# Distance products in two row groups of 32 rows instead of one product over 128 rows, with the factors copied to both groups by ScalarE

## The chip, the cores and the metric

The kernel runs on one core of one Trainium2 chip (trn2). The metric is the device time of one execution in microseconds (us). Three runs of the kernel before took 588.64, 587.37 and 587.83 us; their median is 587.83 us.

## The reference

Sixteen graphs of 512 nodes with 128 features go through four graph layers, each followed by a residual sum and a layer norm, `x = layernorm(x + layer(x))`. The layer that matters here is the last one, a gated unit with a neighbourhood built from distances:

```python
s = x @ w_se.T + b_se                                     # 512 x 3 per graph
sq = jnp.sum(s * s, axis=-1)
dist = sq[:, :, None] + sq[:, None, :] - 2.0 * jnp.einsum('bnd,bmd->bnm', s, s)
A = jnp.exp(-dist) * mask                                 # mask is the adjacency
msg = jax.nn.relu(x @ w_msg.T + b_msg)
x_nmp = jnp.einsum('bnm,bmd->bnd', A, msg)
```

Beside it the same layer has a convolution over 17 neighbouring nodes and a gate with three sigmoid and tanh parts. The first layer multiplies by the adjacency (512 x 512), the third by an attention weighted with it.

## The kernel before, in words

A first part works out the second layer for the first 25 nodes of all graphs, and prepares weights. The main part, `turn`, then runs once for each step of a software pipeline: graph g is in its last layer (`cur`), while graph g+1 is in its first and third layer (`nxt`), graph g+2 is loaded and transposed (`new`), and graph g-1 is finished (`prev`). `over_graphs` writes out the first turn and the last ones and makes a hardware loop of two turns a pass of the others. Sixteen turns have `cur`; one more only finishes the last graph. Each engine has its own instruction list, in the order in which it is written, and semaphores tie the lists together (`wait(engine, semaphore, value)`).

Products of full precision are made of three products of float32r operands (`three`, L255 to L259): high times high, high times low and low times high. So most of TensorE's instructions carry the lines L257, L258 and L259.

The distance matrix of a graph, 512 x 512, is four products, one for each chunk `mc` of 128 rows. For these VectorE writes `G` (L1465 to L1477): for each node 13 numbers for the left factor and 13 for the right one, made of the high and the low parts of `s` and of its half squared length, so that the product of the two is minus half the distance. Left and right numbers lie 32 columns apart (`KD` = 13 numbers, `GR` = 32). Four transposing products (L1711) turn `G` into `SQ_BANK`, left factors in partitions 0 to 12 and right factors in partitions 32 to 44. ScalarE copies both to `LR`, to partitions 0 to 12, as left half `LR[:, 0, :]` and right half `LR[:, 1, :]` (L1234, L1235). All other partitions of `LR` were set to zero once, at the start (L1129), and `distances(mc)` (L1604 to L1606) multiplies over all 128 partitions, into `AT_BANK[0]` for even chunks and `AT_BANK[1]` for odd ones.

TensorE's order in one turn around the change is: transposes of `x3`, first aggregation over the adjacency (twelve products of 512 columns), `CONV1`, `hn`, L1684, L1696, L1702, the nine even taps of the convolution (27 products of 256 columns), L1711, nine more taps (27 products), **distances(0) and distances(1)**, six of the eight odd taps (18 products), the second aggregation (twelve products of 512 columns, L1735 to L1740), **distances(2) and distances(3)**, the last two odd taps (6 products), L1752, L1760, transposes of the adjacency, and the gates. In front of the second aggregation TensorE waits for the weighted features of the graph in its third layer: their high part `x_hi` comes from ScalarE (L1243), their low part `x_lo` from VectorE (L1521, L1524), which in its turn needs the chain that begins behind L1684.

ScalarE's order there is: L1228, L1229 (messages), wait for L1711, L1234, L1235, then a wait for VectorE's `ef` and the exponential L1239, four scalings L1243, L1248, and the exponentials of the first two distance products (L1182). VectorE multiplies each exponential by the transposed adjacency (L1354), and TensorE multiplies that by the messages (L1760).

Of the kernel before, what the change touches and what calls it, by code (L numbers as in the profile page):

```python
# [32 lines left out]
KD = 13  # L33
GR = 32
# [4 lines left out]
def network_kernel(nc, a, out):  # L39
# [3 lines left out]
    ACT = mybir.ActivationFunctionType  # L43
# [3 lines left out]
    with ctx:  # L47
        def sb(name, shape, dt=f32):
            return ctx.enter_context(nc.sbuf_tensor(name, shape, dt))

        def sem(name):
            return ctx.enter_context(nc.semaphore(name))
# [14 lines left out]
        AT_BANK = [bank[0], bank[1]]  # L67
# [4 lines left out]
        SQ_BANK = bank[6]  # L72
# [123 lines left out]
        LR = sb("LR", [128, 2, N], f32r)  # L196
# [17 lines left out]
        def ms_banks(nxt):  # L214
            return (MS_BANK if nxt else AG_BANK, AT_BANK[0])

        def ms_half(o):
            return o[:, 0:2 * DM].rearrange("p (c d) -> p c d", c=2)[:, :, 0:D]
# [4 lines left out]
        def wait(eng, s, count):  # L223

            if not (isinstance(count, int) and count <= 0):
                eng.wait_ge(s, count)
# [28 lines left out]
        def three(pe, o, lh, ll, rh, rl, start, stop):  # L255

            nc.tensor.matmul(o, lh, rh, start=start, stop=False)  # L257
            nc.tensor.matmul(o, lh, rl, start=False, stop=False)  # L258
            return nc.tensor.matmul(o, ll, rh, start=False, stop=stop)  # L259

        def ch(c):
            return slice(c * 128, (c + 1) * 128)
# [69 lines left out]
        with nc.Block() as block:  # L332
# [742 lines left out]
        dv_s, dv_ssq, dv_q, dv_shi, dv_qh, dv_G, pe_LR, ac_LR = [sem(n) for n in (  # L1075
            "dv_s", "dv_ssq", "dv_q", "dv_shi", "dv_qh", "dv_G", "pe_LR", "ac_LR")]
# [91 lines left out]
        def _(act):  # L1168
            s = nc.scalar
            def turn(V, dma, par, graph, has, outs):  # L1170
# [48 lines left out]
                if cur:  # L1219
                    wait(act, pe_hn, V(1))  # L1220
                    wait(act, ac_nn, V(0))
                    s.activation(gh, HN_BANK[:, :], ACT.Identity, bias=gate_bias[:, 2:3], scale=0.5).then_inc(ac_gh, 1)
                    wait(act, po_cd, V(1))
                    wait(act, pe_P1, V(0))
                    s.activation(cd_hi[:, :, :], cd[:, :, :], ACT.Identity).then_inc(ac_cdh, 1)
                    wait(act, dv_s, V(1))
                    wait(act, pe_N, V(0))
                    s.activation(msg_v[1], ms_half(ms_banks(nxt)[1]), ACT.Relu).then_inc(ac_msx, 1)  # L1228
                    s.activation(msg_v[0], ms_half(ms_banks(nxt)[0]), ACT.Relu).then_inc(ac_msg, 1)  # L1229
                    wait(act, pe_LR, V(1))  # L1230
                    if not prev:
                        act.wait_ge(po_LR0, 1)
                    wait(act, pe_D[NC - 1], V(0))
                    s.activation(LR[0:KD, 0, :], SQ_BANK[0:KD, :], ACT.Identity)  # L1234
                    s.activation(LR[0:KD, 1, :], SQ_BANK[GR:GR + KD, :], ACT.Identity).then_inc(ac_LR, 1)  # L1235
                if nxt:
                    wait(act, dv_f, V(2))
                    wait(act, dv_pf, V(1))
# [12 lines left out]
                if prev and cur:  # L1251
# [3 lines left out]
                    for c in range(NC):  # L1255
                        last = s.activation(y_out[:, c, :], X_BANK[:, ch(c)], ACT.Identity, bias=shift[:, c:c + 1],
                                            scale=rs[3][:, c:c + 1])
# [31 lines left out]
                if new:  # L1289
                    split_adjacency(3)  # L1290

            over_graphs(act, turn)

        @block.vector
# [292 lines left out]
        def _(pe):  # L1587
            t_ = nc.tensor
            def turn(V, dma, par, graph, has, outs):
# [12 lines left out]
                    return last  # L1602

                def distances(mc):  # L1604
                    t_.matmul(AT_BANK[mc % 2][:, :], LR[:, 0, ch(mc)], LR[:, 1, :], start=True, stop=True  # L1605
                              ).then_inc(pe_D[mc], 1)  # L1606

                def some_taps(o, first, count, hi, lo, ks):
# [24 lines left out]
                if prev and not cur:  # L1633
# [15 lines left out]
                    for h in range(2):  # L1649
                        pe.wait_ge(dv_gy, V(0) + h)  # L1650
                        for c in range(2):
                            last = t_.transpose(Y_HALF[h][:, ch(c)], gy[:, ch(2 * h + c)], ident[:, :])
                        last.then_inc(pe_yT, 1)
                    return
                if cur:
                    wait(pe, dv_x3, V(1))
                    wait(pe, dv_nmplo, V(0))
                    for c in range(NC):
                        last = t_.transpose(X_BANK[:, ch(c)], x3[:, c, :], ident[:, :])  # L1659
# [21 lines left out]
                if nxt:  # L1681
                    wait(pe, ac_agg1, V(2))
                    for c in range(NC):
                        last = t_.matmul(AG_BANK[:, ch(c)], agg_sb[:, ch(c)], w0[:, :], start=True, stop=True)  # L1684
                    last.then_inc(pe_out0, 1)
                if cur:
# [7 lines left out]
                    for c in range(NC):  # L1694
                        o = ms_banks(nxt)[c // 2]
                        last = t_.matmul(o[:, DM * (c % 2):DM * (c % 2) + D + 3], x3M[:, ch(c)], wmsT,  # L1696
                                         start=True, stop=True)
                    last.then_inc(pe_ms, 1)
                if prev and nxt:
                    wait(pe, dv_gy, V(0))  # L1700
                    for c in range(NC):
                        last = t_.transpose(X_BANK[:, ch(c)], gy[:, ch(c)], ident[:, :])  # L1702
                    last.then_inc(pe_yT, 1)
                if cur:
# [5 lines left out]
                    for c in range(NC):  # L1710
                        last = t_.matmul(SQ_BANK[0:2 * GR, ch(c)], G[:, c, :, :].rearrange("p k g -> p (k g)"), ident_r[:, :],  # L1711
                                         start=True, stop=True)
                    last.then_inc(pe_LR, 1)
                if prev and not nxt:
                    wait(pe, dv_gy, V(0))
                    for c in range(NC):
                        last = t_.transpose(X_BANK[:, ch(c)], gy[:, ch(c)], ident[:, :])
# [5 lines left out]
                if cur:  # L1723
                    wait(pe, ac_LR, V(1))
                    wait(pe, ac_msx, V(1))
                    for mc in range(2):
                        if nxt:
                            wait(pe, dv_aTlo[3 - 2 * mc], V(2))
                        wait(pe, dv_P[mc + 2], V(0))
                        distances(mc)  # L1730
                    wait(pe, ac_gh, V(1))
                    some_taps(HN_BANK[:, 0:HALF], EVEN, ODD, cd_hi[:, 1, :], cd_lo[:, 1, :], range(ODD - 2))
                if nxt:
                    wait(pe, dv_pf, V(2))
                    for mc in range(NC):  # L1735
                        wait(pe, ac_xs[mc], V(2))
                        wait(pe, dv_xs[mc], V(2))
                        last = three(pe, AG_BANK[:, :], x_hi[:, mc, :], x_lo[:, mc, :], aT_hi[:, mc, :],
                                     aT_lo[:, mc, :], mc == 0, mc == NC - 1)
                    last.then_inc(pe_agg2, 1)  # L1740
                if cur:
                    for mc in range(2, NC):
                        wait(pe, dv_P[mc - 2], V(1))
                        distances(mc)
                    some_taps(HN_BANK[:, 0:HALF], EVEN, ODD, cd_hi[:, 1, :], cd_lo[:, 1, :], range(ODD - 2, ODD)
                              ).then_inc(pe_P1, 1)
                if nxt:
# [3 lines left out]
                    for c in range(NC):  # L1751
                        last = t_.matmul(OUT2[:, c // 2, c % 2, :], agg_sb[:, ch(c)], wwT, start=True, stop=True)  # L1752
                    last.then_inc(pe_out2, 1)
                if cur:
# [3 lines left out]
                    for mc in range(NC):  # L1758
                        wait(pe, dv_P[mc], V(1))
                        last = t_.matmul(X_BANK[:, :], msg[:, ch(mc)], P[:, mc, :], start=(mc == 0), stop=(mc == NC - 1))  # L1760
# [40 lines left out]
```

## Time and profile before

| | |
|---|---|
| median of three runs | 587.83 us (587.37 to 588.64) |
| the profiled execution | 587.87 us, of which the trace spans 586.1 us |
| TensorE (PE) | 568.1 us busy, 97% of the span |
| weight loads of TensorE (PEld) | 488.0 us |
| VectorE (DVE) | 476.6 us, 81% |
| ScalarE (ACT) | 341.3 us, 58% |
| GpSimd (POOL) | 120.7 us, 21% |

PE rows are products, PEld rows the loads of their stationary operand, which lie beside the product before. A row of the timeline gives a start, the time from the start of its first instruction to the end of its last, engine, line, operation, output <- inputs, rows * columns of the array that are active, the shape and how many instructions were merged into the row (x5). The ends of products are modelled and consecutive products overlap in the record, so what a product costs is read from the distance between starts. For a merged row of n equal products that distance is (length of the row - length of one) / (n - 1).

### The profile page before, as it was taken

Reading aid. Unit: us, or ns where it says so; the run is one execution under the profiler, and the core shown is the slowest. Engines: PE = TensorE matmul, PEld = TensorE weight load, DVE = VectorE, ACT = ScalarE, POOL = GpSimd, SP = SyncE. Lnnn points to the kernel's source line nnn. Section 1 sums busy time; section 2 is a strip of 40 time slices with the busy share of each in tenths; the row PEclk is TensorE's granted clock in tenths of the full one; section 3 lists DMA queues with packets and bytes.
Section 4 is the critical chain, followed back from the end, with each engine's and each line's share of the span. In section 5 each row is a group of like instructions: output and inputs, shape, how many; then the busy total and the mean of one; then the engine's idle time right before and its main releaser. Section 6 shows DMA issues by size and latency. Waiting matters only on the chain.

```text
span 586.1 us, 11733 instructions
## 1 busy us (share of the span) xinstructions
PE 568.1 (97%) x3579; PEld 488.0 (83%) x3579; DVE 476.6 (81%) x1798; ACT 341.3 (58%) x716; POOL 120.7 (21%) x140
## 2 busy tenths in 40 slices
PE   7998999999999999999999999999999999999894
PEld 6896987878979797979888897979797988889684
DVE  4778868888888888888888888888888888888665
ACT  2306646557575656675665757566657566575442
POOL 3310130312213030212131221303021313122110
PEclk9999999999999999999999999999999999999998
DMA  8980032030120303030303012030303030000000
GB/s 187 292 289 2 2 115 82 2 110 1 39 71 1 107 0 108 0 108 0 108 0 95 13 29 79 0 108 0 108 0 108 0 108 1 20 2 19 1 19 18
DMA packets 33300, 34.46 MB, mean 59 GB/s; under 512 B 1663, under 2 KB 22531, under 8 KB 33146
## 3 DMA queue, kind: packets, MB, share of 16 engines
q1 hardware_dynamic: 32986, 34.01, 18.5%
q8 instruction: 13, 0.21, 0.1%
q10 hardware_dynamic: 288, 0.13, 0.1%
q14 instruction: 13, 0.11, 0.1%
HBM read 29.74 MB, written 4.39 MB: 58 GB/s over the span
## 4 chain that ended last, share of the span: by engine, by line
PE 85%; DVE 1%; ACT 0%; issue 0%; POOLq 0%; POOL 0%; DVEq 0%
PE bank L257 14%; PE bank L258 13%; PE bank L259 13%; PE bank L1760 9%; PE pair L257 6%; PE pair L259 6%; PE pair L258 6%; PE bank L1594 4%; PE bank L1605 3%; PE bank L1696 2%; PE pair L1752 2%; PE pair L1684 2%; PE bank L1659 1%; PE bank L1702 1%; PE pair L1711 1%
## 5 line engine op out<-in xcount | busy, mean ns | idle before, releaser
L1133 POOL TENSOR_TENSOR rs<-ve,neg_half 128x4 f32<-128x4 f32 (+1 forms) x60 | 57.2, 953 | 279.1 <-DVE ve L1322 246.3
L257 PE MATMUL bank<-cd_hi,w_hi 128*128 128x256 f32 x272 | 77.5, 285 | 0.0
L258 PE MATMUL bank<-cd_lo,w_hi 128*128 128x256 f32 x272 | 76.7, 282 | 0.0
L259 PE MATMUL bank<-cd_hi,w_lo 128*128 128x256 f32 x272 | 76.5, 281 | 0.0
L1760 PE MATMUL bank<-P,msg 128*128 128x512 f32 x128 | 57.6, 592 | 0.0
L257 PE MATMUL pair<-aT_hi,x_hi 128*128 128x512 f32 x128 | 52.5, 410 | 0.6 <-DVE x_lo L776 0.3
L257 PEld LDWEIGHTS bank<-cd_hi,w_hi 128*128 128x128 f32 x272 | 51.3, 189 | 1.6
L258 PEld LDWEIGHTS bank<-cd_lo,w_hi 128*128 128x128 f32 x272 | 51.4, 189 | 1.4
L259 PEld LDWEIGHTS bank<-cd_hi,w_lo 128*128 128x128 f32 x272 | 51.3, 189 | 0.0
L259 PE MATMUL pair<-aT_hi,x_lo 128*128 128x512 f32 x128 | 50.2, 392 | 0.0
L258 PE MATMUL pair<-aT_lo,x_hi 128*128 128x512 f32 x128 | 50.0, 391 | 0.0
L1354 DVE TENSOR_TENSOR P<-bank,aT 128x512 f32<-128x512 f32 x64 | 41.1, 685 | 9.2 <-ACT bank L1182 9.1
L1341 DVE TENSOR_TENSOR aT_lo<-bank,aT_hi 128x512 fp32r<-128x512 f32 x56 | 38.5, 687 | 8.0 <-ACT aT L1178 8.0
L1176 ACT ACTIVATE aT_hi<-bank 128x512 fp32r<-128x512 f32 x56 | 34.4, 614 | 16.5 <-PE bank L1594 16.5
L1760 PEld LDWEIGHTS bank<-P,msg 128*128 128x128 f32 x128 | 23.1, 190 | 23.0 <-issue 23.0
L257 PE MATMUL bank<-co_hi,w_hi 128*128 128x256 f32 x144 | 41.9, 291 | 0.0
L258 PE MATMUL bank<-co_lo,w_hi 128*128 128x256 f32 x144 | 40.4, 281 | 0.0
L259 PE MATMUL bank<-co_hi,w_lo 128*128 128x256 f32 x144 | 40.4, 280 | 0.0
L1143 POOL TENSOR_TENSOR x<-x_nat,bias 128x512 f32<-128x512 f32 x15 | 19.7, 1316 | 76.6 <-DVE x3T_lo L1429 76.6
L1178 ACT ACTIVATE aT<-bank 128x512 f32<-128x512 f32 x56 | 34.7, 620 | 0.0
L1182 ACT ACTIVATE bank<-bank 128x512 f32<-128x512 f32 x64 | 34.4, 574 | 0.0
L1594 PEld LDWEIGHTS bank<-ident,adj_nat 128*128 128x128 f32 x224 | 26.2, 141 | 9.4 <-issue 7.4
(363 smaller groups left out, 1540.0 us busy)
## 6 DMA issues: line engine op xcount, KB each, us to landing
adj_nat<-in_adj_dram SPq DMA_DIRECT2D x16, 1024.0 KB, 6.1
x_nat<-in_x_dram SPq DMA_DIRECT2D x16, 256.0 KB, 2.9
xt<-in_x_dram SPq DMA_DIRECT2D x3, 1280.0 KB, 11.8
out_dram<-y_out SPq DMA_DIRECT2D x15, 256.0 KB, 2.2
hw<-in_L_gnn_W_dram SPq DMA_DIRECT2D x2, 640.0 KB, 6.9
xt<-in_L_gnn_conv_w_dram SPq DMA_DIRECT2D x1, 1088.0 KB, 9.7
aT<-in_adj_dram SPq DMA_DIRECT2D x5, 96.0 KB
nat_ih<-in_L_gnn_w_ih_dram SPq DMA_DIRECT2D x1, 384.0 KB, 5.4
```

The costliest lines, as they stand in the source:

```text
L257: nc.tensor.matmul(o, lh, rh, start=start, stop=False)
L258: nc.tensor.matmul(o, lh, rl, start=False, stop=False)
L259: return nc.tensor.matmul(o, ll, rh, start=False, stop=stop)
L1133: g.tensor_tensor(rs[i][:, 0:n], ve[i][:, 0:n], neg_half[:, 0:n], ALU.pow).then_inc(po_rs[i], 1)
L1143: g.tensor_tensor(x1[:, :, :], x_nat[1 - par][:, :, :], bc(bias0[:, :], NC), ALU.add).then_inc(po_xb, 1)
L1176: s.activation(aT_hi[:, mc, :], AT_OF[mc][:, :], ACT.Identity)
L1178: s.activation(aT[par][:, mc, :], AT_OF[mc][:, :], ACT.Identity).then_inc(ac_aT[mc], 1)
L1182: s.activation(AT_BANK[mc % 2][:, :], AT_BANK[mc % 2][:, :], ACT.Exp, scale=2.0).then_inc(ac_E[mc], 1)
L1341: v.tensor_tensor(aT_lo[:, mc, :], AT_OF[mc][:, :], f(aT_hi[:, mc, :]), ALU.subtract).then_inc(dv_aTlo[mc], 1)
L1354: v.tensor_tensor(P[:, mc, :], AT_BANK[mc % 2][:, :], aT[par][:, mc, :], ALU.mult).then_inc(dv_P[mc], 1)
L1594: last = t_.transpose(AT_OF[mc][:, ch(c)], adj_nat[par][:, c, ch(mc)], ident[:, :])
L1760: last = t_.matmul(X_BANK[:, :], msg[:, ch(mc)], P[:, mc, :], start=(mc == 0), stop=(mc == NC - 1))
```

## The change

The factors are copied twice, to partitions 0 to 12 and to partitions 32 to 44 of `LR` (four ScalarE copies in place of two), and each distance product runs over 32 partitions only: even chunks over partitions 0 to 31, odd chunks over partitions 32 to 63. The outputs, the semaphores and the order of all engines stay as they are.

```diff
@@ ScalarE
                     wait(act, pe_D[NC - 1], V(0))
-                    s.activation(LR[0:KD, 0, :], SQ_BANK[0:KD, :], ACT.Identity)
-                    s.activation(LR[0:KD, 1, :], SQ_BANK[GR:GR + KD, :], ACT.Identity).then_inc(ac_LR, 1)
+                    for k in range(2):
+                        for i in range(2):
+                            last = s.activation(LR[GR * k:GR * k + KD, i, :], SQ_BANK[GR * i:GR * i + KD, :], ACT.Identity)
+                    last.then_inc(ac_LR, 1)
@@ TensorE
                 def distances(mc):
-                    t_.matmul(AT_BANK[mc % 2][:, :], LR[:, 0, ch(mc)], LR[:, 1, :], start=True, stop=True
+                    k = slice(GR * (mc % 2), GR * (mc % 2 + 1))
+                    t_.matmul(AT_BANK[mc % 2][:, :], LR[k, 0, ch(mc)], LR[k, 1, :], start=True, stop=True
                               ).then_inc(pe_D[mc], 1)
```

## Rows read from the trace of the kernel before

**Rows 1.** The page: busy time of each engine, share of the span, instructions; then the granted clock in 40 slices, tenths.

```profile
PE 568.1 (97%) x3579; PEld 488.0 (83%) x3579; DVE 476.6 (81%) x1798; ACT 341.3 (58%) x716; POOL 120.7 (21%) x140
...
PEclk9999999999999999999999999999999999999998
```

**Rows 2.** The page: shares of the chain of waits, by engine.

```profile
PE 85%; DVE 1%; ACT 0%; issue 0%; POOLq 0%; POOL 0%; DVEq 0%
```

**Rows 3.** The distance products' line: durations in ns (least, median, most).

```profile
L1605 PE MATMUL bank<-LR x64: 391/395/398, 88.4 to 567.5; 128*128 128x512 f32 x64
```

**Rows 4.** Timeline, TensorE, around the first pair of one turn.

```profile
279.42 0.28 PE L259 MATMUL bank<-cd_hi,w_lo 128*128 128x256 f32 x1
279.53 0.62 PE L1605 MATMUL bank<-LR 128*128 128x512 f32 x2
280.00 0.28 PE L257 MATMUL bank<-cd_hi,w_hi 128*128 128x256 f32 x1
```

**Rows 5.** Timeline, TensorE, around the second pair of the same turn.

```profile
284.79 0.39 PE L259 MATMUL pair<-aT_hi,x_lo 128*128 128x512 f32 x1
285.02 0.63 PE L1605 MATMUL bank<-LR 128*128 128x512 f32 x2
285.49 0.28 PE L257 MATMUL bank<-cd_hi,w_hi 128*128 128x256 f32 x1
```

**Rows 6.** Timeline, TensorE, 23.4 to 24.5: a product over 25 rows.

```profile
23.16 0.72 PE L874 MATMUL bank<-aPT,xt 128*128 128x100 f32 x5
23.81 0.48 PE L966 MATMUL pair<-nadjT,x 25*128 25x125 f32 x2
24.22 0.47 PE L874 MATMUL bank<-aPT,xt 128*128 128x100 f32 x2
```

**Rows 7.** Timeline, weight loads, 23.4 to 24.5.

```profile
23.81 0.29 PEld L966 LDWEIGHTS pair<-nadjT,x 25*128 25x128 f32 x2
24.22 0.41 PEld L874 LDWEIGHTS bank<-aPT,xt 128*128 128x128 f32 x3
```

**Rows 8.** Timeline, 32.3 to 34.0: products, then the first load over 25 rows.

```profile
32.04 0.50 PE L874 MATMUL bank<-aPT,xt 128*128 128x100 f32 x3
...
32.47 0.78 PEld L998 LDWEIGHTS bank<-prod,nadjT 25*25 25x25 f32 x8
```

**Rows 9.** Timeline, 275.8 to 276.6: float32r products with 64 active columns.

```profile
275.90 0.28 PE L259 MATMUL bank<-co_hi,w_lo 128*128 128x256 f32 x1
276.02 0.39 PE L1711 MATMUL pair<-ident_r,G 128*64 128x128 f32 x4
276.26 0.33 PE L257 MATMUL bank<-cd_hi,w_hi 128*128 128x256 f32 x1
```

**Rows 10.** Timeline, weight loads at the second aggregation's head, three turns.

```profile
281.91 0.19 PEld L259 LDWEIGHTS bank<-cd_hi,w_lo 128*128 128x128 f32 x1
282.15 0.19 PEld L257 LDWEIGHTS pair<-aT_hi,x_hi 128*128 128x128 f32 x1
...
186.34 0.19 PEld L259 LDWEIGHTS bank<-cd_hi,w_lo 128*128 128x128 f32 x1
186.68 0.19 PEld L257 LDWEIGHTS pair<-aT_hi,x_hi 128*128 128x128 f32 x1 [0.15 <-issue]
...
122.50 0.19 PEld L259 LDWEIGHTS bank<-cd_hi,w_lo 128*128 128x128 f32 x1
122.97 0.19 PEld L257 LDWEIGHTS pair<-aT_hi,x_hi 128*128 128x128 f32 x1 [0.28 <-issue]
```

**Rows 11.** Timeline, ScalarE, from 276 in the same turn.

```profile
276.45 0.59 ACT L1234 ACTIVATE LR<-pair 13x512 fp32r<-13x512 f32 x1 [1.44 <-PE pair L1711]
277.06 0.59 ACT L1235 ACTIVATE LR<-pair 13x512 fp32r<-13x512 f32 x1
279.84 0.30 ACT L1239 ACTIVATE pef<-ef,c 128x4 f32<-128x4 f32 x1 [2.19 <-DVE ef L1358]
```

**Rows 12.** Waits of ScalarE: total us, times, longest.

```profile
ACT pef L1239 <- DVE ef L1358: 34.1, 15, 2.6
```

## The prediction

> **What bounds the kernel now.** I read the page first: TensorE is busy 97% of the span, VectorE 81%, ScalarE 58%, and the granted clock is full (2.4 GHz) in all slices [rows 1]. The chain of waits then says that TensorE holds 85% of the chain that ended last, all other engines together some 1% [rows 2]. So time added to TensorE's stream is added to the span, unless it falls where TensorE waits anyway. To find such places I went through the timeline of TensorE and of its weight loads. In the steady turns every load starts with the product before it and is hidden behind it, except at the head of the second aggregation: there a load normally 0.12 us behind the last one comes 0.24 us behind it in one turn (282.15 after 281.91), 0.34 in another, 0.47 in a third [rows 10]. TensorE waits there for the features that VectorE and ScalarE scale. These three stand for three kinds. Of the 15 turns with this aggregation 8 wait 0.12 to 0.14 us, 5 wait 0.22 to 0.23, one 0.35, and the first turn none: 8 x 0.12 + 5 x 0.22 + 0.35 = 2.4 us in all.
>
> **What the distance products cost now.** There are 64 [rows 3], in 32 pairs, two pairs in each of 16 turns. Around the first pair TensorE's starts are 279.42 (last tap), 279.53, and 280.00 for the next tap [rows 4]; the pair takes 0.47 us. Around the second they are 285.02 and 285.49, again 0.47 [rows 5]. One product of the pair so takes 0.23 us: with 512 columns it is the streaming that counts, not how many rows hold data. Two that ran side by side in two row groups could save at most that 0.23 us a pair, 32 x 0.23 = 7.4 us.
>
> **What a change from 128 rows to 32 costs.** The program before has a few products over 25 rows between products over 128, in its first part. TensorE's starts there: five L874 products take 0.72 us with a last one of some 0.275, so they are (0.72 - 0.275) / 4 = 0.11 apart and the last starts at 23.61. The first load over 25 rows comes at 23.81, 0.20 us behind that start, and not with it [rows 6, 7]. Some 9 us later the same: the last of three L874 products starts at 32.04 + 0.50 - 0.275 = 32.265, the next load over 25 rows at 32.47, 0.205 behind [rows 8]. The way back is alike: the second 25-row product starts at 23.81 + 0.48 - 0.27 = 24.02, the next load over 128 rows at 24.22, 0.20 behind [rows 6, 7]. I read this as: when the number of rows changes, the next load does not start until the array has run empty, and is then exposed. The price from starts: from the last product before to the second product over 25 rows it is 24.02 - 23.61 = 0.41 us where two ordinary steps take 0.22, so **entry 0.19 us**. From there to the second product over 128 rows, which starts at 24.22 + 0.47 - 0.275 = 24.415, it is 0.395 where two steps take 0.22, so **exit 0.17 us**.
>
> A visit costs 0.36 us by this. Ends for it: above, 0.40, if each end costs the full 0.20 us from the product's start to the load; below, nothing, by the nearest float32r row. The four float32r products with only 64 active columns (L1711) start 0.12 us behind the tap before them, an ordinary step [rows 9], so for float32r a smaller number of columns alone empties nothing. The distance products are float32r too, but what changes in them is the rows, as in [rows 6 to 8]; I take 0.36.
>
> The Trainium skill has a rule that speaks against the change: the page "TensorEngine Tiling (Array Packing)", section "Key Properties", says that changing the tiling mode, not only the tile, drains TensorE. The trace agrees with it for float32, by the 0.20 us of [rows 6 to 8], and no row before shows it for float32r with fewer rows.
>
> **What the two row groups give back.** No row shows two products in different row groups. Below, nothing: the second starts 0.23 us behind the first as now. Above, 0.23: both start together. Between them lies the load: a product needs its own, and behind an exposed load the next load starts about 0.11 us later (the two 25-row loads take 0.29 us together and one some 0.18, so 0.11 apart [rows 7]). If the second product may start as soon as its load is in, it starts 0.11 us behind the first, and 0.23 - 0.11 = 0.12 us is saved. I take **0.12**; the nearest rows make the load the next limit once the streaming is not. The visit is then 0.36 - 0.12 = 0.24 us dearer than now, 32 x 0.24 = 7.7 us.
>
> By the Trainium skill ("TensorE: Matmul & The Clock Gate", section "Measured speedup vs the span model") products in different row groups start about 4 ns apart; the saving would be the full 0.23 us of the upper end, which is the third rival below.
>
> **What is taken in by waits.** The first pair of a turn lies ahead of the second aggregation. TensorE arrives there 0.24 us later, and the chain of VectorE and ScalarE that it waits for (it begins behind L1684, before the pair) is not moved. So the waits listed above go first: 8 x 0.12 + 5 x 0.22 + 0.24 = 2.3 us. What is late next is TensorE itself. Behind the second pair there is no such wait; its exponentials and what VectorE makes of them come later by what TensorE is late, and no more.
>
> **The copies.** Two more copies of 0.59 us a turn, 32 in all, 19 us of ScalarE. In the turn shown the last copy ends at 277.65 and the first distance load starts at 279.42 [rows 4, 11]: 1.8 us of room for 2 x 0.6 = 1.2. Behind them in ScalarE's queue stands the exponential L1239, for which ScalarE waits 2.19 us here and 34.1 / 15 = 2.3 us on average [rows 11, 12]; that wait covers the copies, and 1.0 us is left. So I cost them at nothing. Without this cover each 1.2 us would hold up the scaled features and with them TensorE, 15 x 1.2 = 18 us at most. The bank that they read is next written long after, and that product waits for the same semaphore already.
>
> **Sum.** 7.7 - 2.3 = +5.4 us on the profiled execution's 587.87 us, which is its span of 586.1 and 1.8 around it, and which stands at the median of the runs shown (587.83). Forecast: 593.3 us.
>
> **Rivals.**
> - Emptying, but no overlap: the second product waits for the first as now. Each visit costs 0.36; 32 x 0.36 = 11.5, less 2.4 of waits: +9.1, 597.0 us. For it: all products of the trace before run one behind the other. Against: they all share the same rows.
> - Emptying, and both products at once (saving 0.23): a visit costs 0.13, 32 x 0.13 = 4.2, less 14 x 0.12 = 1.7: +2.4, 590.2 us. Against: two loads must be done first, and the rows show them 0.11 apart.
> - **Faster**: float32r does not empty the array when rows change, as it doesn't with 64 columns [rows 9], and the pair overlaps by 0.12 to 0.23. First pairs then gain only in the two turns without the wait of [rows 10], since TensorE would reach a wait sooner; the second pairs gain in all 16. 18 x 0.12 = 2.2 to 18 x 0.23 = 4.1: 583.7 to 585.7 us, say 585. It decides from the point at which entry and exit together cost less than the overlap gives, at most 0.23 us; the rows with fewer rows say 0.36.
> - The change does nothing: no emptying and no overlap, or the two equal. 587.8 us.
>
> **How the numbers follow.** Forecast 0.42, no overlap 0.20, both at once 0.10, faster 0.14, nothing 0.14. Less than 0.2% (1.2 us) can't be told from no change by a measurement of this kernel. Slower by more than that: 0.42 + 0.20 + 0.10 = 0.72; within: 0.14; faster: 0.14. The range leaves out the faster case and the upper tail (the 0.40 visit without overlap would be 32 x 0.40 - 2.4 = +10.4, 598.3): 587 to 598.5 us.
>
> **What would show it.** Right: the loads of both distance products read 32 active rows; the first one starts not with the product before but 0.2 us or more behind its start (more for the second pair, where 512 columns stand before it in place of 256); the tap behind a pair shows the same; from the start of the last product before to the second tap behind it the timeline is 0.24 us longer than the 0.70 of now (280.00 - 279.42 [rows 4] and one step of 0.12); the waits at the aggregation's head are gone or short; ScalarE's wait before L1239 is down to about 1.1 us. The two products' starts tell the rivals apart: 0.11 apart for the forecast, 0.23 for no overlap, near zero for both at once. Wrong: a distance load that starts with the product before it, or an exponential L1239 that comes late because of the copies.

## The result, and the profile after

The changed kernel is slower. Its median of seven runs is 591.71 us (589.35 to 592.45) against 587.37 us (586.63 to 588.64) in seven runs of the kernel before beside them; the ratio of the two is 1.0054, with a 95% interval of 1.0028 to 1.0080. Run again later on, beside other kernels, it gave 590.63 us against 587.07 and a ratio of 1.0048 (1.0028 to 1.0068). So the change costs about 0.5%, 3 us by these ratios; the medians alone are 4.3 and 3.6 us apart, in which the granted clock may have a part (last section). The forecast was 593.3 us, which is +5.4 us, with a range of 587 to 598.5.

The page of the changed kernel, the lines that answer to [rows 1, 2]:

```profile
span 588.0 us, 11765 instructions
PE 570.3 (97%) x3579; PEld 480.6 (82%) x3579; DVE 476.3 (81%) x1798; ACT 360.1 (61%) x748; POOL 120.6 (21%) x140
...
PE 85%; DVE 1%; ACT 0%; issue 0%; POOLq 0%; POOL 0%; DVEq 0%
```

TensorE is still what the chain runs through. ScalarE is busy 19 us longer (360.1 against 341.3), the 32 new copies.

The timeline of the changed kernel around the first pair of one turn, products and then weight loads (start, length of the row, engine, line, operation, output <- inputs, rows * columns active, shape, how many; it answers to [rows 4]):

```profile
279.38 0.28 PE L259 MATMUL bank<-cd_hi,w_lo 128*128 128x256 f32 x1
279.59 0.50 PE L1608 MATMUL bank<-LR 32*128 32x512 f32 x2
280.02 0.39 PE L257 MATMUL bank<-cd_hi,w_hi 128*128 128x256 f32 x1
280.25 0.28 PE L258 MATMUL bank<-cd_lo,w_hi 128*128 128x256 f32 x1
...
279.59 0.18 PEld L1608 LDWEIGHTS bank<-LR 32*128 32x128 f32 x2
280.02 0.19 PEld L257 LDWEIGHTS bank<-cd_hi,w_hi 128*128 128x128 f32 x1 [0.25 <-issue]
```

Three things are to be seen. The first load over 32 rows comes 0.21 us behind the start of the last tap and no longer with it; I read this as the array running empty first. The two loads together take no longer than one (0.18 us), and the two products take 0.50 us together where one takes 0.497: both start at once, 3 to 4 ns apart in the trace. And the load of the next tap comes 0.43 us behind the two, exposed again. From the last tap before (279.38) to the second tap behind (280.25) it is 0.87 us where it was 0.70, so this visit costs 0.17 us.

Around the second pair, where 512 columns stand in front (it answers to [rows 5]):

```profile
284.77 0.39 PE L259 MATMUL pair<-aT_hi,x_lo 128*128 128x512 f32 x1
285.09 0.50 PE L1608 MATMUL bank<-LR 32*128 32x512 f32 x2
285.52 0.39 PE L257 MATMUL bank<-cd_hi,w_hi 128*128 128x256 f32 x1
285.75 0.29 PE L258 MATMUL bank<-cd_lo,w_hi 128*128 128x256 f32 x1
```

The first product comes 0.32 us behind the one before. The stretch is 0.98 us; before, it was 285.49 - 284.79 = 0.70 [rows 5] and a step of 0.12, so 0.82. This visit costs 0.16 us (0.154 in the trace's own ns, 0.167 for the first pair). The delay of the load grows with what is still streaming: 0.21 us behind a product of 256 columns, 0.32 behind one of 512, and the steps of these two are 0.12 and 0.23 us. A fixed price of a change of rows would not grow so; a wait until the products in front have ended would.

The line of the distance products as a whole, durations in ns (least, median, most), says that all 64 are alike, with 32 rows, one length of load and one of product:

```profile
L1608 PEld LDWEIGHTS bank<-LR x64: 181/181/182, 87.3 to 569.1; 32*128 32x128 f32 x64
L1608 PE MATMUL bank<-LR x64: 491/497/501, 87.3 to 569.1; 32*128 32x512 f32 x64
```

ScalarE, the stretch that answers to [rows 11]:

```profile
276.42 2.39 ACT L1236 ACTIVATE LR<-pair 13x512 fp32r<-13x512 f32 x4 [1.44 <-PE pair L1714]
279.80 0.30 ACT L1241 ACTIVATE pef<-ef,c 128x4 f32<-128x4 f32 x1 [0.99 <-DVE ef L1360]
```

The copies end at 278.81, and ScalarE still waits 0.99 us for VectorE (before: 2.19). Their cover holds.

**Turns as a measure.** Whole times of one kernel differ from run to run by about as much as this change costs (589.35 to 592.45 us above). The distance from one turn to the same place in a later one is steadier: two traces of the changed kernel give 32.029 and 32.043 us a turn. I take the four products of L1711 (L1714 in the changed kernel) in the second and in the fifteenth turn, 13 turns apart. The changed kernel:

```profile
115.72 0.40 PE L1714 MATMUL pair<-ident_r,G 128*64 128x128 f32 x4
...
532.10 0.39 PE L1714 MATMUL pair<-ident_r,G 128*64 128x128 f32 x4
```

and the kernel before:

```profile
116.62 0.40 PE L1711 MATMUL pair<-ident_r,G 128*64 128x128 f32 x4
...
530.69 0.39 PE L1711 MATMUL pair<-ident_r,G 128*64 128x128 f32 x4
```

That is (532.10 - 115.72) / 13 = 32.029 us a turn against (530.69 - 116.62) / 13 = 31.852: 0.177 us more, 2.8 us over 16 turns. The two spans differ by only 1.9 us because the first part, up to this place in the first turn, is 1.2 us shorter in the trace after (83.54 against 84.75 us); nothing in it was changed. Behind it the trace after is 3.1 us longer (504.4 against 501.4): the step from the first turn to the second, outside the 13, has grown by 0.30 us, since the first turn has no wait that could take anything in.

### The profile page after: what moved, and what is told of

Read it like the earlier page. It is cut to its first block, busy times and chain, and to the rows that moved or that the text cites. A ratio compares the mean times of both kernels' runs of the same rounds, so it can differ in the third digit from the quotient of the medians.

```text
span 588.0 us, 11765 instructions
## 1 busy us (share of the span) xinstructions
PE 570.3 (97%) x3579; PEld 480.6 (82%) x3579; DVE 476.3 (81%) x1798; ACT 360.1 (61%) x748; POOL 120.6 (21%) x140
## 4 chain that ended last, share of the span: by engine, by line
PE 85%; DVE 1%; ACT 0%; issue 0%; POOLq 0%; POOL 0%; DVEq 0%
PE bank L257 15%; PE bank L259 13%; PE bank L258 13%; PE bank L1763 9%; PE pair L257 6%; PE pair L259 6%; PE pair L258 6%; PE bank L1596 4%; PE bank L1699 2%; PE bank L1608 2%; PE pair L1755 2%; PE pair L1687 2%; PE bank L1662 1%; PE bank L1705 1%; PE pair L1714 1%
## 5 line engine op out<-in xcount | busy, mean ns | idle before, releaser
L257 PE MATMUL bank<-cd_hi,w_hi 128*128 128x256 f32 x272 | 80.7, 297 | 0.0
L1236 ACT ACTIVATE LR<-pair 13x512 fp32r<-13x512 f32 x64 | 37.6, 588 | 24.0 <-PE pair L1714 23.4
```

What stands on the lines that cost most here:

```text
L1236: last = s.activation(LR[GR * k:GR * k + KD, i, :], SQ_BANK[GR * i:GR * i + KD, :], ACT.Identity)
```

## The experiments

The table has for each kernel its median, the ratio to the kernel before with its interval, and the length of a turn from its trace; the kernel before had medians of 587.07 to 587.59 us beside them.

```
kernel              median us  ratio to before (95%)      turn us
before              587.07                                31.852
changed, again      590.63     1.0048 (1.0028 to 1.0068)  32.043
same_group          597.28     1.0161 (1.0129 to 1.0192)  32.438
copies_alone        586.93     0.9999 (0.9982 to 1.0016)  31.849
rows64              596.67     1.0162 (1.0129 to 1.0196)  32.452
first_pair          588.04     1.0009 (0.9982 to 1.0035)  31.866
second_pair         589.87     1.0028 (1.0006 to 1.0051)  32.010
moved               584.89     0.9946 (0.9925 to 0.9967)  31.692
moved, again        585.27     0.9967 (0.9954 to 0.9980)  31.704
three_one_copy      584.04     0.9945 (0.9929 to 0.9961)  31.679
three_six_copies    593.49     1.0107 (1.0086 to 1.0128)  32.190
```

**The changed kernel again.**

> The changed kernel once more, unaltered, beside three variants of it. All theories: a time between 589 and 592.5 us, as in its first runs (589.35 to 592.45). In the trace a distance load 0.21 us behind the start of the tap before it, both distance products within 0.01 us of each other, and 32.03 us from the first pair of one turn to that of the next (before: 31.85). If the 1.9 us that the first trace is longer than the trace before is not the whole of the change, this run shows by how much the turns alone are longer: 0.18 us each, some 3 us in all.

Measured: 590.63 us, turn of 32.043 us, 0.19 us more than before, 3.1 us in 16 turns. As expected.

**same_group**: both products of a pair over the same 32 rows.

```diff
-                    k = slice(GR * (mc % 2), GR * (mc % 2 + 1))
+                    k = slice(0, GR)
```

> Both products of a pair run over rows 0 to 31, so that nothing can run side by side; the change of rows stays. Theory A (the array empties at each change of rows, 0.36 us a visit, and the second row group gives back the 0.23 us of one product, so 0.16 net with a little lost): second product 0.23 us behind the first, a visit 0.38 us longer than before, 2 x 0.38 less some 0.17 of wait taken in = 0.6 us a turn, 16 turns: about +9.5 us over the kernel before, 597 us. Theory B (the two products were not really side by side, the record only models it): starts and time as in the changed kernel, 589 to 592.5 us.

Measured: 597.28 us. The timeline around a first pair:

```profile
282.55 0.28 PE L259 MATMUL bank<-cd_hi,w_lo 128*128 128x256 f32 x1
282.76 0.73 PE L1608 MATMUL bank<-LR 32*128 32x512 f32 x2
283.41 0.39 PE L257 MATMUL bank<-cd_hi,w_hi 128*128 128x256 f32 x1
283.64 0.28 PE L258 MATMUL bank<-cd_lo,w_hi 128*128 128x256 f32 x1
...
282.75 0.29 PEld L1608 LDWEIGHTS bank<-LR 32*128 32x128 f32 x2
```

From the last tap before to the second behind: 1.09 us, against 0.70 before the change and 0.87 in the changed kernel. So a visit without overlap costs 0.39 us, and the second row group gives back 0.22 of it. The overlap is real: theory B fails, and theory A holds. It expected 0.6 us a turn and 597 us; measured are 32.438 - 31.852 = 0.59 us a turn and 597.28 us.

**copies_alone**: the copies of the change, the products over 128 rows.

```diff
-                    k = slice(GR * (mc % 2), GR * (mc % 2 + 1))
+                    k = slice(0, 128)
...
-                    ... ACT.Exp, scale=2.0)
+                    ... ACT.Exp, scale=1.0)
```

> Four copies as in the changed kernel, but both products over all 128 rows; each sum then holds both copies, twice the value, and the exponential's scale is 1.0 in place of 2.0, so the output is the same. Theory A (the rows are the price, the copies are hidden behind ScalarE's wait of 2.2 us): time of the kernel before, 586.6 to 588.6 us, turn of 31.85 us. Theory C (the copies hold up the scaled features): turn of 32.0 us and 590 us or more.

Measured: 586.93 us and 31.849 us a turn. No cost of the copies is to be seen (ratio 0.9999, 0.9982 to 1.0016; ScalarE still waits 1.00 us before its exponential, L1241 here), so theory C is out.

**rows64**: two copies, both products over rows 0 to 63.

```diff
 from the kernel before
-                    t_.matmul(AT_BANK[mc % 2][:, :], LR[:, 0, ch(mc)], LR[:, 1, :], start=True, stop=True
+                    k = slice(0, 2 * GR)
+                    t_.matmul(AT_BANK[mc % 2][:, :], LR[k, 0, ch(mc)], LR[k, 1, :], start=True, stop=True
```

> Two copies as before, both products over rows 0 to 63 (rows 13 to 63 are zero). Theory A (any change in the number of rows empties the array): loads 0.2 us late as with 32 rows, products 0.23 apart, as same_group, about 597 us. Theory D (only groups of 32 rows are another mode for the array): as the kernel before, 587.5 us.

Measured: 596.67 us, 32.452 us a turn, the same as same_group within what two runs differ. Around a first pair:

```profile
283.38 0.28 PE L259 MATMUL bank<-cd_hi,w_lo 128*128 128x256 f32 x1
283.59 0.73 PE L1606 MATMUL bank<-LR 64*128 64x512 f32 x2
284.25 0.39 PE L257 MATMUL bank<-cd_hi,w_hi 128*128 128x256 f32 x1
284.47 0.28 PE L258 MATMUL bank<-cd_lo,w_hi 128*128 128x256 f32 x1
```

The stretch is 1.09 us again. The change of rows has its price with 64 rows as with 32 (theory D fails), and copies have no part in it, since this kernel has only two.

**first_pair and second_pair**: the row groups for one pair only.

```diff
 first_pair
+                    k = slice(GR * mc, GR * (mc + 1)) if mc < 2 else slice(0, 128)
+                    ... ACT.Exp, scale=2.0 if mc < 2 else 1.0)
 second_pair
+                    k = slice(GR * (mc - 2), GR * (mc - 1)) if mc > 1 else slice(0, 128)
+                    ... ACT.Exp, scale=1.0 if mc < 2 else 2.0)
```

> Four copies; only the first pair of a turn (chunks 0 and 1) runs in two row groups, the second pair over all 128 rows (there each sum holds both copies, and the exponential's scale is halved for it, so the output is the same). Theory A (0.16 us a visit, but ahead of the second aggregation TensorE waits 0.12 to 0.35 us in 14 of 15 turns before the change, and that wait takes it in): within 1 us of the kernel before, turn of 31.85 to 31.88 us. Theory E (the wait moves along with TensorE, nothing is taken in): turn of 32.01 us, +2.5 us. The other pair is run the other way round in the next kernel; the sum of both should be the changed kernel.

> The mirror of the kernel first_pair: only chunks 2 and 3 run in two row groups. Theory A (behind the second pair nothing waits, so 0.155 us a turn are lost in full): turn of 32.0 us, 16 x 0.155 = +2.5 us over the kernel before. Theory E (both pairs cost the same): also +2.5 us, and then first_pair shows +2.5 us as well and the changed kernel's +3.5 us is less than the sum.

Measured: first_pair 31.866 us a turn, 0.014 over the kernel before, though each of its visits costs 0.17 us in the timeline; its time can't be told from the kernel before (1.0009, 0.9982 to 1.0035). second_pair 32.010 us a turn, 0.158 over it, the whole of its visit. The sum of both, 0.172, is the changed kernel's 0.177. So the wait at the head of the second aggregation takes in nearly all of the first pair's cost, and nothing takes in the second's; theory E fails. The weight loads of first_pair at that place, in a turn as in [rows 10]:

```profile
281.85 0.19 PEld L259 LDWEIGHTS bank<-cd_hi,w_lo 128*128 128x128 f32 x1
281.97 0.19 PEld L257 LDWEIGHTS pair<-aT_hi,x_hi 128*128 128x128 f32 x1
```

They are 0.12 us apart, an ordinary step, where they were 0.24. Added up over the 15 turns, what lies beyond such a step is 2.49 us in the trace of the kernel before, 2.49 in second_pair, 0.61 in first_pair and 0.52 in the first trace of the changed kernel.

**moved**: no row groups; distances(2) goes into the wait. From the kernel before:

```diff
+        D_OF = [bank[0], bank[1], MS_BANK, bank[1]]      # in place of AT_BANK[mc % 2], in all three uses
...
                         distances(mc)
+                    wait(pe, ac_msg, V(1))
+                    distances(2)
                     wait(pe, ac_gh, V(1))
...
-                    for mc in range(2, NC):
-                        wait(pe, dv_P[mc - 2], V(1))
-                        distances(mc)
+                    wait(pe, dv_P[1], V(1))
+                    distances(3)
```

> The kernel before, all products over 128 rows, two copies; distances(2) goes to the bank of the messages, which is free by then, and is issued right behind distances(1), ahead of the second aggregation; distances(3) stays. Theory A (TensorE waits at the head of the aggregation for a chain that it does not carry): 0.23 us of work moves into a wait of 0.12 to 0.35 us, which gives 8 x 0.12 + 5 x 0.22 + 0.23 = 2.3 us: about 585 us, 0.4% under the kernel before, turn of 31.7 us, provided that the later product L1752, now 0.23 us sooner, still finds its copy of the aggregation ready (0.27 us of room). Theory F (the chain of VectorE sets the turn as a whole): the wait comes back elsewhere and the time stays 587 us.

> The kernel moved once more, unaltered, as the ground for the two beside it: 584 to 586 us, turn of 31.69 us.

Measured: 584.89 us, ratio 0.9946 (0.9925 to 0.9967), and again 585.27 us, 0.9967 (0.9954 to 0.9980). It beats the kernel before, and with it the changed one. The two ratios make 3.2 and 1.9 us and the turns 2.6 and 2.4; 2.3 had been worked out. At the head of the second aggregation, weight loads as in [rows 10]:

```profile
281.99 0.19 PEld L260 LDWEIGHTS bank<-cd_hi,w_lo 128*128 128x128 f32 x1
282.10 0.19 PEld L258 LDWEIGHTS pair<-aT_hi,x_hi 128*128 128x128 f32 x1
```

The load comes 0.11 us behind the last one where it was 0.24: the wait is gone here, and over the 15 turns only 0.2 us of the 2.49 are left. Theory F falls.

**three_one_copy and three_six_copies**: moved, with three products in three row groups. three_one_copy leaves out the copies for the second and third group, so that chunks 1 and 2 read zeros and only its time counts.

```diff
+                    k = slice(GR * mc, GR * (mc + 1)) if mc < 3 else slice(0, 128)
+                    t_.matmul(D_OF[mc][:, :], LR[k, 0, ch(mc)], LR[k, 1, :], start=True, stop=True
 and in three_six_copies, for k in range(3), six copies, with a scale of 2.0 / 3.0 for the last exponential
```

> The kernel moved, with its first three products in three row groups (rows 0 to 31, 32 to 63, 64 to 95) and the last over 128 rows. The copies stay at two, so the second and third group hold zeros: the distances of chunks 1 and 2 are left out of the output, and only the time counts. Theory A (a visit has a fixed price of 0.39 us, and each product beyond the first costs nothing, so a third one pays 0.23 more): the three loads start within 0.01 us of each other, and from the last tap before to the second tap behind it is 0.87 us, as for two products in the changed kernel, where three products one behind the other take 0.93. The 0.06 us fall into what is left of the wait at the aggregation's head: turn of 31.66 to 31.69 us, time within 0.2% of moved. Theory G (only two groups can be loaded and run at once): the third product starts 0.11 to 0.23 us behind, and the stretch is 0.98 us or more, time 1 us above moved or more.

> As three_one_copy, with the factors copied to all three groups by six copies, so that the output is whole (the last product sums three copies, and its exponential has a third of the scale). Theory A: six copies take 3.6 us where two take 1.2, and ScalarE's room was 1.8 us beyond the two: TensorE waits 0.6 us for them in each turn, and the exponential L1239 and the scaled features behind them come late too: turn of 32.2 us or more, 16 x 0.5 = +8 us over moved, 593 us. Rival H (the queue of ScalarE has more room than its wait shows): as three_one_copy, 585 us.

The timeline of three_one_copy, products and then loads:

```profile
278.00 0.28 PE L260 MATMUL bank<-cd_hi,w_lo 128*128 128x256 f32 x1
278.20 0.50 PE L1607 MATMUL bank<-LR 32*128 32x512 f32 x3
278.64 0.39 PE L258 MATMUL bank<-cd_hi,w_hi 128*128 128x256 f32 x1
278.86 0.28 PE L259 MATMUL bank<-cd_lo,w_hi 128*128 128x256 f32 x1
...
278.20 0.19 PEld L1607 LDWEIGHTS bank<-LR 32*128 32x128 f32 x3
```

Three products take the same 0.50 us as two, and the stretch of 0.86 us is that of the pair. A third product is free once the visit is paid, and theory G falls. The stretch is 0.06 us shorter than in moved (0.93), but whether the kernel gains by it is not shown: its turn of 31.679 us is 0.013 and 0.025 under the two traces of moved, which differ by 0.012 themselves, and the times (584.04 and 585.27 us, ratios 0.9945 and 0.9967 with intervals that overlap) don't tell them apart.

With all six copies any gain is lost many times over: 593.49 us. Who waited for whom, TensorE (total us, times, longest), and its timeline around the three products of one turn:

```profile
PE bank L1609 <- ACT LR L1237: 5.7, 15, 0.4
...
283.65 0.28 PE L260 MATMUL bank<-cd_hi,w_lo 128*128 128x256 f32 x1
284.33 0.59 PE L1609 MATMUL bank<-LR 32*128 32x512 f32 x3 [0.40 <-ACT LR L1237]
284.85 0.39 PE L258 MATMUL bank<-cd_hi,w_hi 128*128 128x256 f32 x1
285.07 0.28 PE L259 MATMUL bank<-cd_lo,w_hi 128*128 128x256 f32 x1
```

TensorE now waits 0.4 us a turn for the copies, where 0.6 had been expected: that estimate left out the 0.2 us by which the load is late anyway, and 0.6 - 0.2 = 0.4. The first product starts 0.68 us behind the last tap in place of 0.20, the three are no longer all side by side (0.59 us in place of 0.50), and the stretch is 1.42 us in place of 0.86. The turn is 0.51 us longer than in three_one_copy. The cover that made four copies free was 1.8 us, as read from [rows 4, 11], and the next two overran it. The expectation of 32.2 us or more a turn and 593 us holds (32.190 measured), and rival H falls.

## Why the prediction was right, and where it was off

The direction, the emptying at each change of rows, the part of the loss that the wait takes in, and the hidden copies hold. The step that says how far the two products overlap does not, and with it the size: forecast were +5.4 us, and the turns, the wait and the times agree on about +3. The forecast of 593.3 us is 1.6 us over the first median and 2.7 over the second; of the nearness to the first a part is luck, since that median fell among the four of seven runs with the lower mean clock (last section). The rival "both at once", with 590.2 us and a chance of 0.10, was the nearer one, in mechanism and in time, and the range held both.

- **Entry and exit**, put at 0.19 + 0.17 = 0.36 us from a 25-row product in float32 [rows 6, 7]. Measured without overlap (same_group): 0.39. There the second product starts 0.54 us behind the last tap where it was 0.35, so 0.19 to enter, and the rest, 0.20, is the way back; the exit was put 0.03 too low. Rows of another type and another length were good to a tenth. The two 25-row products and their two loads come from one call (L966), which the working took for two. The open point, whether float32r empties the array at all, since with 64 columns it does not [rows 9], is settled: it does, for 32 rows and for 64.
- **The overlap**, put at 0.12 us because a load had to follow a load 0.11 us later [rows 7]. This is the term that was mis-sized. The sign given for the forecast was two products 0.11 us apart; they start 3 to 4 ns apart, and so do their loads. Loads into different row groups go side by side, and the overlap gives 0.39 - 0.17 = 0.22 us, the upper end (0.23). The rows that I leaned on showed two loads into the same rows, where the one does have to wait for the other; in same_group the second load is 0.11 us behind again (two take 0.29 us together, one 0.18). The rival "both products at once" (the second in the list of rivals) was the true case here. By the Trainium skill ("TensorE: Matmul & The Clock Gate", "Measured speedup vs the span model") the products start about 4 ns apart. The trace agrees, with 3 to 4 ns.
- **The visit** so costs 0.16 us and not 0.24, nor the 0.13 of that rival, whose emptying was a little too cheap: 32 x 0.16 = 5.1 us. (The rival's sum is a little off too: 4.2 - 1.7 is 2.5, not 2.4.)
- **The wait**, put at 2.3 us for a visit of 0.24. With 0.167 the same working gives 8 x 0.12 + 6 x 0.167 = 2.0; first_pair shows 0.167 - 0.014 = 0.153 a turn, 2.1 us in 14 turns, and the loads at the aggregation's head show 2.49 - 0.52 = 1.97 us taken in. 5.1 less 2.0 to 2.1 is 3.0 to 3.1 us, against 3.1 us in the traces behind the first part and the ratios of 1.0048 to 1.0054, which make 2.8 to 3.2.
- **The copies**, put at nothing with 1.8 us of room: shown by copies_alone, and the size of the room by three_six_copies.
- **The clock** was called full in all slices, but the last digit of [rows 1] is an 8, and the trace of the kernel before holds a stretch at the lower level, shown in the last section. It is in both first traces alike and changes nothing in the comparison of turns.
- The faster rival needed a change of rows that costs less than the overlap gives. It costs 0.39 against 0.22; with three products it is 0.39 against 0.45, and the visit is shorter by those 0.06 us, but only with the copies left out.

## What to carry to other kernels

Row groups are bought by the visit, not by the product: here 0.39 us to leave the 128 rows and come back, and 0.22 us back for each product of 512 columns beyond the first. In this stream, whose weight loads are otherwise hidden, two such products don't pay. Three save 0.06 us in the timeline of the visit, no gain in time was shown for them, and the copies that they need cost far more. Where TensorE waits a little for another engine in each turn, first look for work behind the wait that could stand ahead of it: one product moved into a free bank gave 2 to 3 us, and no regrouping gave that.

## What the runs showed that I had not expected

Two weight loads into different row groups take the time of one (0.18 us for two, 0.19 for three), and so do the products.

The granted clock falls to its lower level, 1.2 GHz, for one short stretch near the end in some executions and not in others. In the trace of the kernel before, three stretches read (engines' busy time in order of the page, then the granted clock, DMA share and GB/s):

```profile
551.00:554.00 3.00, 1.05 (x7) 0.75 (x6) 2.12 (x4) 2.31 (x4) 0.00 (x0) 1.00 0.00 0
554.50:558.00 3.50, 3.50 (x16) 3.22 (x15) 2.22 (x4) 2.30 (x4) 1.12 (x1) 0.52 0.00 0
558.00:561.00 3.00, 3.00 (x30) 3.00 (x28) 1.60 (x11) 0.81 (x3) 0.00 (x0) 1.00 0.00 0
```

The clock is at 0.52 in the middle one, with TensorE busy throughout; in the stretch ahead it was busy for only 1.05 of 3 us, as it waits there 1.95 us for ScalarE's x3T. The changed kernel's second trace has that wait too but no such stretch of clock behind it, and from L1714 of the fifteenth turn to that of the sixteenth it takes 29.08 us, where its first trace, with the stretch, takes 30.25. That is 1.2 us of difference between two executions of one kernel, more than a third of what this change costs, and the reason to compare turns and not spans. Why the clock falls in one and not in the other is not shown.

The times show it too. In the first seven runs of the changed kernel the mean granted clock is 0.993 to 0.996 in the three of 589.35 to 589.72 us, and 0.989 to 0.991 in the four of 591.71 to 592.45 us. Runs of one clock compare better: beside each other, in the second measurement, those at 0.993 have medians of 590.92 and 587.76 us (3.2 us apart, four and five runs), those at 0.996 of 588.76 and 586.39 us (2.4 us apart, three and eight runs).
